# Presetting semaphores from five engines, moving the preparation's gates, and carrying routing scores with the tensor engine

## The reference

```
ga = (2 * (ga >= 0) - 1) * jnp.maximum(jnp.abs(ga), 0.25)
gb = (2 * (gb >= 0) - 1) * jnp.maximum(jnp.abs(gb), 0.25)
```

```
router_scores = softmax(xt @ Wr + br)
fs = where(mask, router_scores, 0.0); fs = fs / (fs.sum(-1) + 1e-06)
h = silu(up) * gate * fs[:, :, None]
out = einsum('teh,ehd->td', h, Wdown) + fs @ bdown
```

## Time and profile before

| | |
|---|---|
| three runs, median (lowest to highest) | 1050.38 us (1047.12 to 1051.72) |
| profiled execution, its own time | 1048.9 us |
| its span | 1047.2 us |
| busy in the span: PE, DVE, ACT, POOL | 850.5, 735.4, 458.7, 198.5 us |
| preparation and the start | 0 to 50.6 us |
| attention | 50.6 to 400.2 us |
| routing | 400.2 to 622.0 us |
| experts | 622.0 to 803.7 us |
| second layer's attention, then its network | 803.7 to 885.2, 885.2 to 1047.2 us |

### The profile page before, as it was taken

The page is one execution under the profiler, slowest core; times in us unless marked ns, Lnnn a source line. Parts: engine busy times, 40 slices in busy tenths (PEclk is TensorE's granted clock), DMA queues, the critical chain, the costliest instruction groups (busy, mean ns, idle before and its releaser), DMA issues. The chain is left out here.

```text
span 1047.2 us, 19509 instructions
## 1 busy us (share of the span) xinstructions
PE 850.5 (81%) x7216; PEld 481.2 (46%) x7216; DVE 735.4 (70%) x1376; ACT 458.7 (44%) x812; POOL 198.5 (19%) x160
## 2 busy tenths in 40 slices
PE   7289999999889973999986859999996984667574
PEld 4167667666556641344432323333443752344342
DVE  3524546788878777999885758888883443787875
ACT  4445656556555442677766840111112354222222
POOL 3042000000000001000005645445440000224230
PEclk9679999999989896999997989999997997788788
DMA  4072000000000000577847599888880000000001
GB/s 124 5 114 43 2 2 3 3 2 2 3 2 3 2 2 1 231 282 301 300 162 302 211 313 362 286 302 281 300 302 0 1 1 1 1 10 11 20 11 31
DMA packets 54056, 113.40 MB, mean 108 GB/s; under 512 B 14352, under 2 KB 28496, under 8 KB 53840
## 3 DMA queue, kind: packets, MB, share of 16 engines
q1 hardware_dynamic: 45360, 109.07, 30.0%
q10 hardware_dynamic: 8608, 3.15, 1.2%
HBM read 57.68 MB, written 52.43 MB: 105 GB/s over the span
## 5 line engine op out<-in xcount | busy, mean ns | idle before, releaser
L1218 PE MATMUL bank<-so_made,Wd 128*128 128x512 f32 x256 | 130.5, 599 | 7.1 <-DVE so_made L1279 6.7
L1279 DVE TENSOR_TENSOR so_made<-so_ug,bank 128x512 f32<-128x512 f32 x128 | 84.3, 673 | 27.4 <-PE bank L1204 10.0
L1183 POOL TENSOR_TENSOR so_ug<-so_ug 128x512 f32<-128x512 f32 x64 | 82.4, 1287 | 92.1 <-DMA so_ug<-hidden 92.1
L909 ACT ACTIVATE att_qk<-bank 128x512 f32<-128x512 f32 x128 | 66.9, 603 | 45.7 <-PE bank L712 45.4
L746 PE MATMUL bank<-att_qk 64*128 64x128 f32 x1024 | 78.2, 294 | 0.0
L997 DVE TENSOR_TENSOR att_am<-bank,causal 128x512 f32<-128x512 f32 x64 | 44.0, 688 | 45.7 <-PE bank L746 45.7
L746 PEld LDWEIGHTS bank<-att_qk 64*128 64x128 f32 x1024 | 65.6, 196 | 20.4 <-issue 20.4
L1218 PEld LDWEIGHTS bank<-so_made,Wd 128*128 128x128 f32 x256 | 46.8, 190 | 59.4 <-issue 29.2
L1456 POOL TENSOR_TENSOR so_made<-so_ug 128x512 f32<-128x512 f32 x23 | 41.7, 1830 | 164.5 <-DVE so_cnt L1656 146.0
L1479 ACT ACTIVATE so_off<-bank,bu 128x512 f32<-128x512 f32 x64 | 43.9, 686 | 38.2 <-PE bank L57 23.8
L1429 POOL MEMSET so_below<- 128x128 f16 x1 | 0.2, 207 | 315.3 <-POOLq L141 315.3
(11 more groups left out here) (399 smaller groups left out, 1937.9 us busy)
## 6 DMA issues: line engine op xcount, KB each, us to landing
so_ug<-hidden SPq DMA_DIRECT2D x64, 768.0 KB, 4.8
hidden<-so_off SPq DMA_DIRECT2D x64, 512.0 KB, 3.1
hidden<-so_made SPq DMA_DIRECT2D x64, 256.0 KB, 2.1
prep_xin<-in_L_attn_x_dram ACTq DMA_DIRECT2D x8, 256.0 KB, 8.8
out_dram<-ff_ot SPq DMA_DIRECT2D x8, 256.0 KB, 2.3
so_other<-so_key SPq DMA_DIRECT2D x2, 512.0 KB, 5.6
prep_wm<-in_L_wmod_dram SPq DMA_DIRECT2D x2, 384.0 KB, 6.1
F<-so_fhi ACTq DMA_DIRECT2D x4, 128.0 KB, 4.7
```

Source lines behind the costliest of these rows:

```text
L909: nc.scalar.activation(qk[t % 2][:, r, :, :].rearrange("p a l -> p (a l)"), psF[r], ACT.Relu).then_inc(s_["fe"], 1)
L1183: nc.gpsimd.tensor_tensor(u, u, g, ALU.mult).then_inc(s_pp, 1)
L1218: nc.tensor.matmul(psY[j][:, :], Wd[:, n, :], hh[n % 4][:], start=False, stop=n == EBLK - 1).then_inc(s_dn[n % 4], 1)
L1279: nc.vector.tensor_tensor(hh[i][:], pg[four % 2][:, i // 2 * 3 + i % 2, :], psW[k % 4][:, :], ALU.mult).then_inc(s_hh[k % 4], 1)
```

## The change

Three parts.

1. `stand` deals the presets out in turn to SP, ACT, DVE, POOL and PE. The routing stage has one semaphore more than before, the attention one more.
2. In the preparation DVE splits `w0` before h instead of after, h_full, h_low and normalise of the first three tiles are in another order, and the 12 small operations leave the preparation. They stand in the attention's `weights(1)`, at the end of chunk 1, and raise a semaphore `gates` that ACT waits for in `gated`. Their tensors `bo`, `sgn` and `mag` become permanent.
3. The DMAs into `F2` go away. DVE, ACT and PE handle the scores in two pieces, 512 and 1536 columns. PE moves them: a matmul with a 64-column half of `swap` copies one token half of one part to its rows of bank 6 or 7, four such matmuls of 256 columns fill a tile of 512 tokens (`to_experts`), and ACT copies the bank into `F2` (`taken`). The first piece gives tiles 0 and 1 before the first tile of experts; `beside` puts the second piece's steps into the first tile: `choose`, `scores`, `low_parts` on DVE behind blocks 1, 3 and 7, and six `to_experts` on PE in rounds 12 to 17. PE begins tile 0 when the first `taken` is done and tile 1 when all eight are.

```diff
             def stand(dma=()):
-                for h in taken:
-                    nc.sync.sem_inc(h, 16 if h in dma else FIRST)
+                engines = (nc.sync, nc.scalar, nc.vector, nc.gpsimd, nc.tensor)
+                for i, h in enumerate(taken):
+                    engines[i % len(engines)].sem_inc(h, 16 if h in dma else FIRST)
                 nc.all_engine_barrier()
...
-                    for u in range(NU):
-                        if u + 5 < NU:
-                            normalise(u + 5)
-                        h_full(u)
-                        if u > 0:
-                            h_low(u - 1)
-                    h_low(NU - 1)
                     dve.wait_ge(s_["load"], 16 + n_load["load"])
                     step(nc.vector.tensor_scalar(Wqkv[0][:], w0[:], WS, None, ALU.mult))
                     step(nc.vector.scalar_tensor_tensor(Wqkv[1][:], w0[:], WS, Wqkv[0][:], ALU.mult, ALU.subtract))
-                    step(nc.vector.tensor_scalar(mod[:, :, 4, :], mod[:, :, 4, :], 1.0, None, ALU.add))
...
+                    for u in range(3):
+                        h_full(u)
+                        h_low(u)
+                        normalise(u + 5)
+                    for u in range(3, NU):
+                        h_full(u)
+                        if u > 3:
+                            h_low(u - 1)
+                    h_low(NU - 1)
...
                         def gated(s):
+                            act.wait_ge(s_["gates"], FIRST + 1)
...
+                            if t == 1:
+
+                                prepare(nc.vector.tensor_scalar(mod[:, :, 4, :], mod[:, :, 4, :], 1.0, None, ALU.add))
+                                for j in (2, 5):
+                                    gate = mod[:, :, j, :]
+                                    prepare(nc.vector.tensor_scalar(sgn[:], gate, 0.0, 2.0, ALU.is_ge, ALU.mult))
+                                    prepare(nc.vector.scalar_tensor_tensor(mag[:], gate, -1.0, gate, ALU.mult, ALU.max))
...
+                        if before is None:
+                            beside(pe, k)
...
-                        act.dma_start(dst[:, :, h, :], src[E * h:E * h + E, cols].rearrange(
-                            "p (c t) -> p c t", t=P)).then_inc(s_f2[half], 16)
...
+                PIECES = ((0, ST), (ST, W))
...
+                def to_experts(pe, n):
+
+                    i = 0 if n < 2 else 1
+                    pe.wait_ge(s_f, FIRST + i + 1)
+                    pe.wait_ge(s_fl, FIRST + i + 1)
+                    if n > 1:
+                        pe.wait_ge(s_F, FIRST + n - 1)
+                    for part, src in enumerate((fhi, flo)):
+                        out = slice(E * part, E * part + E)
+                        for h in range(2):
+                            of_half = swap[:, E - E * h:2 * E - E * h]
+                            m = nc.tensor.matmul(
+                                bank[6 + n % 2][out, :].rearrange("p (c a t) -> p c a t", a=2, t=P)[:, :, h, :],
+                                of_half, src[:, n * ST // 2:(n + 1) * ST // 2].rearrange("p (c t) -> p c t", t=P),
+                                start=True, stop=True, skip_group_check=True, tile_position=(0, E * part))
+                    m.then_inc(s_P, 1)
+
+                def taken(act, n):
+                    act.wait_ge(s_P, FIRST + n + 1)
+                    nc.scalar.copy(F2[:, n * ST:(n + 1) * ST], bank[6 + n % 2]).then_inc(s_F, 1)
+
+                def beside(eng, k):
+
+                    if eng is nc.vector:
+                        if k == 1:
+                            choose(eng, 1)
+                        if k == 3:
+                            scores(eng, 1)
+                        if k == 7:
+                            low_parts(eng, 1)
+                    elif k >= EBLK - 4:
+                        to_experts(eng, k - EBLK + 6)
...
-                        eng.wait_ge(s_f2[what], FIRST + 64)
+                            to_experts(eng, 0)
+                            to_experts(eng, 1)
+                        eng.wait_ge(s_F, FIRST + (1 if what == 0 else T // ST))
```

More of the change, by code:

```diff
@@ L1121, in _, with experts @@
                         add_x(NU - 1)
-        def experts(sem, ug, spare, route_done):
+        def experts(sem, ug, spare, route_done, beside):
             NT, AHEAD, NJ = T // ST, 2, EBLK // 4
@@ L1293, in tile @@
                             h_low(t - 1)
+                        if before is None:
+                            beside(dve, k)
                     upto(dve, s_rec, t * 4 + 4)
@@ L1384, in gate_taken @@
                         eng.wait_ge(s_made, FIRST + kept(m + 1))
-                s_f2 = [sem(f"so_f2{i}") for i in range(2)]
-                def f2_cols(act, half, part):
-                    cols = slice(half * W // 2, (half + 1) * W // 2)
-                    src, s = ((fhi, s_f), (flo, s_fl))[part]
-                    act.wait_ge(s, FIRST + half + 1)
-                    for h in range(2):
-                        dst = F2[E * part:E * part + E, half * T // 2:(half + 1) * T // 2].rearrange(
-                            "p (c a t) -> p c a t", a=2, t=P)
-                        act.dma_start(dst[:, :, h, :], src[E * h:E * h + E, cols].rearrange(
-                            "p (c t) -> p c t", t=P)).then_inc(s_f2[half], 16)
+                PIECES = ((0, ST), (ST, W))
@@ new lines, in route, with choose @@
+                s_P, s_F = sem("so_P"), sem("so_F")
+                def choose(dve, i):
+                    first, end = PIECES[i]
+                    chunks = slice(first // P, end // P)
+                    nc.vector.tensor_tensor(other[:, first:end].rearrange("p (c t) -> p c t", t=P),
+                                            key[0][:, first:end].rearrange("p (c t) -> p c t", t=P),
+                                            nd[:, chunks].unsqueeze(2).to_broadcast([P, (end - first) // P, P]),
+                                            ALU.is_le).then_inc(s_le, 1)
@@ new lines, in scores, with low_parts @@
+                def scores(dve, i):
+                    cols = slice(*PIECES[i])
+                    dve.wait_ge(s_le, FIRST + i + 1)
+                    nc.vector.tensor_tensor(other[:, cols], other[:, cols], from_v[:, cols], ALU.mult).then_inc(s_fd, 1)
+                def low_parts(dve, i):
+                    cols = slice(*PIECES[i])
+                    dve.wait_ge(s_f, FIRST + i + 1)
+                    nc.vector.scalar_tensor_tensor(flo[:, cols], other[:, cols], FS, fhi[:, cols], ALU.mult,
+                                                   ALU.subtract).then_inc(s_fl, 1)
@@ new lines, in high_parts @@
+                def high_parts(act, i):
+                    cols = slice(*PIECES[i])
+                    act.wait_ge(s_fd, FIRST + i + 1)
+                    nc.scalar.activation(fhi[:, cols], other[:, cols], ACT.Identity, scale=FS).then_inc(s_f, 1)
+                def to_experts(pe, n):
[13 more added lines that the diff above has]
+                    m.then_inc(s_P, 1)
@@ L1420, in route @@
                     sem, ug, [t[:] for t in (rt.sq, rt.rs, rt.xn, pads[0], *made)],
-                    route_done)
+                    route_done, beside)
                 stand(dma=s_store + s_off + s_pg)
@@ L1492, in _ @@
                                 act.dma_start(vv[E:P, 1:2], vv[0:E, 0:1]).then_inc(s_vo, 16)
-                        for i in range(2):
-                            cols = slice(i * W // 2, (i + 1) * W // 2)
-                            act.wait_ge(s_fd, FIRST + i + 1)
-                            nc.scalar.activation(fhi[:, cols], other[:, cols], ACT.Identity, scale=FS).then_inc(s_f, 1)
-                            f2_cols(act, i, 0)
-                        for i in range(2):
-                            f2_cols(act, i, 1)
+                        high_parts(act, 0)
+                        for n in range(2):
+                            taken(act, n)
+                        high_parts(act, 1)
+                        for n in range(2, T // ST):
+                            taken(act, n)
                         ex_act(act)
```

41 lines of the change are left out of this document (16 added, 25 removed).

## The result

The changed kernel takes 1046.78 us in the median of 20 executions (1041.63 to 1051.08), the kernel before 1053.51 us on the same chip (1042.38 to 1060.61, 20 executions). The ratio is 0.9944, with a 95% interval of 0.9921 to 0.9967: faster by 5.9 us, where 8.6 were forecast. The profiled execution took 1046.0 us with a span of 1044.3.

What follows compares the result with a forecast made beforehand. No single engine's total decides; only time on the path through the five barrier-separated stages counts. Terms -9.8 - 5.2 + 3.4 + 3.0 = -8.6 us from 1048.9 give 1040.3, with 1.5 for the median 1041.8 us; range 1036.0 to 1048.5.

Steps and rivals of the forecast that it cites:

- Presets, -9.8: Stage starts: five engines raise the presets side by side, PE setting the barrier at 4.3 us; 9.8 us go.
- the rival that they don't: Stage starts: increments from five engines are served one after another, so the presets gain 0; 1051.6 us, chance 0.04.
- What the presets do elsewhere, 0: Outside the stage starts, in routing for instance, dealing out the presets was forecast to change nothing.
- Preparation, -5.2: End of preparation: DVE's reordered work and the removed small operations end the stage at 40.1 instead of 45.29, -5.2 us.
- the bound of -4.3: Preparation's smallest gain, if the split of `w0` delays normalise 7 by its whole length.
- Small operations in the attention, +3.4: Attention, chunk 1: eleven of 12 small DVE operations wait for POOL's 4.08 us operation, delaying PE by 3.4 us.
- the first rival: Small operations slip past POOL and presets run at SP's pace: -13.3 us in sum, 1037.1 us, chance 0.20.
- Part 3, +3.0: Scores moved by PE: loads come 4.4 us earlier, but DVE's operations add 5.3 and PE's matmuls 2.1; +3.0 us.
- PE's share: First tile of experts: PE's 24 matmuls of 256 columns for the scores cost +2.1 us, ends 1.6 and 2.6.
- the rival of the clock: First tile: TensorE's clock stays low, the tile lasts 38.2 us, +14.3; 1056.1 us in all, chance 0.04.
- the worst ends: Sum of all terms at their least favourable ends, given as -1.8 us; it set the range's upper end, 1048.5.
- The rival of the first tile's upper end: First tile: DVE and POOL block each other, loads only 3.3 us earlier; +6.8, sum -4.8, 1045.6 us, chance 0.14.

Runs made afterwards that it cites:

- kernel 9: The kernel before, with every fifth preset raised by PE and the rest by SP; one execution, 1055.27 us.
- kernel 6: The kernel before with presets dealt to five engines, and SP's first expert loads waiting until the first half of the scores has landed; ratio 0.9980.
- kernel 1: The kernel before with only the presets dealt to five engines; ratio 1.0046 to the kernel before.
- 5: The kernel before, unchanged, profiled a second time; one execution, 1052.73 us.

## Why the prediction was right, and where it was not

The direction, the range and the size hold: -5.9 us against -8.6. Its steps hold less well, and two errors lie in it that do not show in the total. That the total came out so near is partly luck, as the sum of the traces at the end of this section shows.

- **Presets, -9.8.** That all engines count at once was right, and the rival that they don't is refuted. The size was off: -7.0. The failing row is the 51 ns of PE's semaphore instruction. I read its length as the added part of its pace and got 0.098 us each; it is 0.156. PE's 44 take 6.9 us instead of 4.3.
- **What the presets do elsewhere, 0.** This is the real miss. "All of it is on the path, since no engine works there" is right for the starts and says nothing of the stream: PE's later instructions all lie up to 44 further on. +2.8 us in routing, in the change too: 2.1 of them in the exchange of `so_vv`, 0.9 behind it, where the reason was not followed. On the kernel before it also turned the order of loads and scores, +5.9 us from ACT's last product to the second tile. How the delay turns the order was not followed either; that PE's 43 semaphores are enough is kernel 9. Behind parts 1 and 2 this stretch is 5.5 us longer than before with the scores on DMA and 4.5 with part 3; on the kernel before it is 0 and 4.9. So the sign of part 3 hangs on the order, as the runs have it as well (-6.3 and +1.8 us), but in both pairs the runs credit part 3 with 3 to 5 us more than its stretch, which the intervals all but allow and no trace explains.
- **Preparation, -5.2.** -4.0 in this pair of traces, less than the bound of -4.3 allowed. The five pairs after the last normalise take 5.37 us, as forecast; the last normalise comes 0.4 us later than before (34.61 against 34.21) although the stage starts 0.7 us earlier. But one pair of traces can't tell more than that: the work of the preparation lasted 41.6 to 44.7 us in the six traces with the old order, 42.5 in the mean, and 36.5 to 38.6 in the seven with the new, 37.7. That is -4.9, close to the forecast, and the last normalise comes 31.5 and 31.7 us after the stage's first work in the mean, so the operations put into the pauses hardly delay the chain.
- **Small operations in the attention, +3.4.** The mechanism was right to the row, and the first rival, that they slip past POOL, is refuted. +2.6. Two of them got in before POOL's long operation, not one, which is 0.2 us of the difference.
- **Part 3, +3.0.** +4.5. The gate was worth 5.1 (4.4 forecast, upper end 5.0), DVE's three operations made the ninth product 5.65 us later (5.3 forecast); both are close. PE's share is the term that failed: +3.9 where I took 2.1 and 2.6 as the end. Six rounds last 0.44 us longer each, 2.6, and the wait for the last copy, 1.00 us at 637.69, is not covered. I had named a cover, the 1.7 us in which PE waits for DVE at a tile's end, and the price without it, 1.1. At the end of the first tile there is no such cover, not even in the kernel before: its PE goes from `Wd` to `spread` at 642.64 and to the column sums at 643.07 without a pause, and waits 0.21 us for DVE after them. Nor do the forecast's numbers for this tile agree with each other: 18.6 + 5.3 + 2.1 is 26.0 us, where the rival of the clock takes 25.2. (Two slips of 0.1 besides: 16 x 1.07 + 2.1 is 19.2, and the worst ends add up to -1.9.)
- **The rival of the clock.** Its condition came true in part: 0.50 in the first stretch of the tile. It costs about 1.8 us, as kernel 6 shows, not 14.3: PE had hardly a pause (3.21 of the first 4 us), and the granted clock was back at 1.00 6.5 us into the tile, close to the six that I had named.
- **The rival of the first tile's upper end** (part 3 at +6.8) was nearer in its sum, 1045.6 us, than the forecast, but by other terms.

What stays open: the terms of the traces sum to -1.1 us (-7.0 - 4.0 + 2.6 + 2.8 + 4.5), and the runs say -5.9 (-8.3 to -3.5 by the interval). The measured sum and the forecast's -8.6 lie on two sides of the runs' -5.9, and the nearness of forecast and result is to that extent luck. With the mean of the preparation instead of this pair's the sum is -2.0. The attention, whose code is the same in all thirteen traces but for the small operations, lasted 338.0 to 346.9 us, and the longer the longer TensorE was at its low clock in it (20.6 to 27.5 us in the five of 338 us, 43.1 in the longest; 35.8 and 26.5 in the two traces of the table, which goes with the -2.5 of its row, although the small operations cost 2.6). The tiles after the first lasted 157.7 to 162.3. Stages like these move a single trace by more than what is left. In which stage the change has the remaining few microseconds on average was not found; no run was aimed at it.

## What to carry to other kernels

Before instructions are added to an engine's stream, even in a place where nobody works, look at what small transfer someone waits for later, and at whether that engine's next instruction fetch may land on it. Where a large and a small group of transfers are under way together, the one that is issued first decides, and removing a delay from the large one can cost more than it gains: force the order with a wait. When work is moved into a wait, put it where the engine waits for something outside (here the 7.2 us in which DVE waits for ACT's last product), not between operations whose consumer is already behind.

## What the runs showed of the hardware

- PE's semaphore increments come 0.156 us apart, DVE's 0.088, POOL's 0.075, ACT's 0.069, SP's 0.063.
- The instruction queue q8 moved 57 packets, 0.93 MB, in the change: 16 KB each. PE and its weight loads have 14,496 instructions, 254 to a packet, so I take these to be PE's. One such packet, met by the `so_vv` exchange of 0.2 KB, made DVE's wait for it 4.6 to 5.0 us instead of 2.6 to 2.7: so in all eight traces of kernels in which PE raises presets, where the packet starts 0.5 to 2.4 us after the first issue, and in none of the other five, where it starts 7.2 us after it. The Trainium skill (Runtime: NRT & Kernel Launch, "Instruction fetch mechanics") says that engines fetch their instructions by DMA in blocks of 16 KiB, 256 instructions, and that the cost of this is mostly hidden. Size and count agree with the trace, 16 KB and 254. It was not hidden from the small transfer that it met.
- A DVE operation of 8 columns that met POOL's `TENSOR_TENSOR` lasted 3.8 to 4.0 us (in the change 3.93), to the end of POOL's, with one SBUF input as with two; with POOL idle it lasted 0.17 us.
- The last four of eight transfers of 128 KB, issued behind loads of 3 MB, held ACT's queue for 9.6 us, and PE, which waited for two of them, began 18.3 us after ACT's last product (kernel 1); where those that it waits for were issued ahead of the loads, it began after 9.1 to 11.0 (kernels 6, 5 and the kernel before).
- TensorE at 0.50 of its clock for the first 6.8 us of a tile, instead of 1.1, made the tile 1.8 us longer (kernel 6).
